# Score products two in a row, then both halves of one maximum product, in the order of TensorE's work

## The reference

```python
q, k, v = x @ Wq + bq, x @ Wk + bk, x @ Wv + bv      # 16 heads of 16 channels
q, k = rope(q), rope(k)
probs = softmax(q @ k.T / 4, axis=-1)                # per head, 2048 x 2048
x = layernorm(x + probs @ v)
r = sigmoid((mu_r * x + (1 - mu_r) * x_prev) @ W_r.T)
k = (mu_k * x + (1 - mu_k) * x_prev) @ W_k.T
out = layernorm(x + r * (square(relu(k)) @ W_v.T))   # x_prev: x one token earlier
```

## Time and profile before

| What | Before |
|---|---|
| Median of three runs | 1656.05 us |
| Profiled execution | 1656.13 us |
| Its span | 1654.3 us |
| TensorE (PE) busy | 1595.5 us, 96% |
| VectorE (DVE) busy | 1443.4 us, 87% |
| ScalarE (ACT) busy | 1168.3 us, 71% |
| Mean granted TensorE clock | 0.975 |

### The profile page before, as it was taken

The page is one execution under the profiler, slowest core; times in us unless marked ns, Lnnn a source line. Parts: engine busy times, 40 slices in busy tenths (PEclk is TensorE's granted clock), DMA queues, the critical chain, the costliest instruction groups (busy, mean ns, idle before and its releaser), DMA issues.

```text
span 1654.3 us, 47865 instructions
## 1 busy us (share of the span) xinstructions
PE 1595.5 (96%) x21312; PEld 683.9 (41%) x21312; DVE 1443.4 (87%) x1491; ACT 1168.3 (71%) x2184; POOL 217.0 (13%) x270
## 2 busy tenths in 40 slices
PE   8858999999999999999999999999999999999997
PEld 4421444444444444444444444444444444443475
DVE  5999888898898898898898998898889989986687
ACT  2441677777777777777777777777777777778542
POOL 4547000000000000000000000000000000001155
PEclk9885899999999999999999999999999999999999
DMA  3344400000000000000000000000000000000011
GB/s 126 114 137 175 129 22 21 22 21 21 21 21 22 21 21 22 21 20 20 18 19 19 17 19 21 21 22 21 21 21 21 21 21 22 2 2 2 1 39 64
DMA packets 36334, 57.70 MB, mean 35 GB/s; under 512 B 5408, under 2 KB 27168, under 8 KB 36128
## 3 DMA queue, kind: packets, MB, share of 16 engines
q1 hardware_dynamic: 34432, 51.53, 9.5%
q10 hardware_dynamic: 1696, 3.12, 0.5%
HBM read 37.46 MB, written 16.78 MB: 33 GB/s over the span
## 4 chain that ended last, share of the span: by engine, by line
PE 85%; DVE 9%; ACT 2%; issue 2%; DMA 1%; SPq 0%; ACTq 0%; POOLq 0%; DVEq 0%; POOL 0%
PE score_ps L547 27%; PE pv_ps L462 27%; PE ring_ps L437 26%; DVE tile_max L938 2%; ACT region L685 2%; DVE ctx_all L879 1%; PE ring_ps L445 1%; DVE region L880 1%; PE score_ps L600 1%; PE ring_ps L511 1%; DMA k_stack<-qk_parts 1%; PE ring_ps L410 1%; DVE ctx_all L878 1%; DVE ctx_all L1013 1%; DVE region L900 1%
## 5 line engine op out<-in xcount | busy, mean ns | idle before, releaser
L938 DVE TENSOR_REDUCE tile_max<-ring_ps 128x1 f32<-128x1024 f32 x1024 | 1207.5, 1220 | 130.6 <-PE ring_ps L437 127.5
L685 ACT ACTIVATE region<-score_ps 128x512 f32<-128x512 f32 x2048 | 1066.9, 602 | 308.1 <-PE score_ps L547 307.5
L437 PE MATMUL ring_ps<-k_stack,q_stack 96*32 96x512 bf16 x8192 | 804.8, 390 | 17.6 <-DMA k_stack<-qk_parts 11.4
L547 PE MATMUL score_ps<-q_stack,k_stack 99*32 99x512 bf16 x8192 | 797.9, 381 | 7.5 <-ACT region L685 3.3
L462 PE MATMUL pv_ps<-region,v_aug 128*32 128x512 f32 x4096 | 529.9, 592 | 0.0
L547 PEld LDWEIGHTS score_ps<-q_stack,k_stack 99*32 99x32 bf16 x8192 | 222.5, 95 | 368.3 <-ACT region L685 183.5
L437 PEld LDWEIGHTS ring_ps<-k_stack,q_stack 96*32 96x32 bf16 x8192 | 219.8, 97 | 356.1 <-DVE tile_max L938 184.7
L462 PEld LDWEIGHTS pv_ps<-region,v_aug 128*32 128x32 f32 x4096 | 125.1, 110 | 103.9 <-ACT region L685 1.6
L813 POOL TENSOR_TENSOR neg_cuts<-neg_max,zeros 128x16 bf16<-128x16 f32 x32 | 7.1, 220 | 888.1 <-DVE neg_max L929 888.1
L410 PE MATMUL ring_ps<-region 128*128 128x512 f32 x128 | 66.5, 674 | 20.0 <-ACT region L651 11.5
L657 ACT ACTIVATE region<-ctx_all 128x2048 bf16<-128x2048 f32 x8 | 15.3, 1910 | 72.4 <-DVE ctx_all L884 52.9
(11 more groups left out here) (70 smaller groups left out, 572.7 us busy)
## 6 DMA issues: line engine op xcount, KB each, us to landing
qk_parts<-region SPq DMA_DIRECT2D x8, 1536.0 KB, 7.5
q_stack<-qk_parts SPq DMA_DIRECT2D x32, 192.0 KB
k_stack<-qk_parts SPq DMA_DIRECT2D x32, 192.0 KB
region<-x_ch SPq DMA_DIRECT2D x8, 512.0 KB, 5.7
q_stack<-qk_parts SPq DMA_DIRECT2D x32, 128.0 KB
k_stack<-qk_parts SPq DMA_DIRECT2D x32, 128.0 KB
region<-x_tok SPq DMA_DIRECT2D x2, 2048.0 KB, 12.6
out<-region SPq DMA_DIRECT2D x8, 512.0 KB, 2.9
```

The costliest lines, as they stand in the source:

```text
L437: mm = pe.matmul(slot[g:g + VCOLS, c * TOK:(c + 1) * TOK], q_stack[0:ROWS, buf, qt * P + g:qt * P + g + VCOLS], k_stack[0:ROWS, buf, lo:lo ...
L547: mm = pe.matmul(score_ps[bank][g:g + VCOLS, :], k_stack[0:ROWS_M, buf, kt * P + g:kt * P + g + VCOLS], q_stack[0:ROWS_M, buf, j * TOK:(j ...
L685: act.activation(probs[:, kt % 2, j, :], score_ps[score_bank(n)[0]][:, :], ACT.Exp, scale=SCALE).then_inc(exps_done, 1)
L938: dve.reduce_max(tile_max[:, parity, unit // 2, unit % 2:unit % 2 + 1], slot[:, :], AX.X)\
```

## The change

The call that issues ring work behind every score product is now made twice behind every second one:

```diff
                         mm.then_inc(scores_ready, 1)
-                        next(work, None)
+                        if j % 2:
+                            next(work, None)
+                            next(work, None)
                         if heads_after == 0:
```

## The result

The changed kernel takes 1687.71 us, the median of four runs (1687.04 to 1687.86), against 1655.98 us for the kernel before. The ratio is 1.0191, with a 95% interval of 1.0173 to 1.0209: slower by 31.7 us. The forecast was 1688.8 us, or 32.8 us slower.

What follows compares the result with a forecast made beforehand. The prediction took TensorE's stream, busy 96% of the span, as the bound. Its terms, 21.8 + 6.6 + 2.3 + 2.1 = 32.8 us, on the profiled 1656.13 us gave 1688.9, or 1688.8 us as a median; range 1682 to 1696.

Steps and rivals of the forecast that it cites:

- The ordinary cycle: 311 cycles without special work: fourth score product waits for the first exponential until 1.15 us; +0.070 us each, 21.8 us.
- Cycle 1: Heads 1 to 30: fourth score product already late, two halves behind it instead of one; +0.219 us each, 6.6 us.
- Cycles 3 and 15: 60 cycles: small wait for VectorE's buffer goes, wait for the exponential comes; +0.038 us each, 2.3 us.
- Cycle 14: 30 heads: first half behind "neg" still waits for VectorE, then the fourth score product is late; +0.070 us, 2.1 us.
- Cycle 13: Third score product has four groups before it in either order and the rest behind it; no change.
- Cycle 2: Transposes delay the score products; the half needing their buffer is due at 611.35, buffer free at 611.33; no cost.
- The maxima's DMAs: Three DMAs issued one group later, landing at most 3.0 us after issue: hidden; if not, 6.6 us in all.
- the score product was not on time: Rival: fourth score product on time, only cycle 1 pays, cycles 3 and 15 gain; 1660.9 us, chance 0.03.
- the ring's waits: Rival, faster: halves' 1.8 us of waits for VectorE go; with 7.7 us from like products, 1646.5 us, chance 0.03.
- exponentials 0.03 us late across the board: Rival: exponential starts at 0.53 us in all 401 gated cycles; 12 us more, 1700.8 us, chance 0.05.
- Like products in a row: Part of the faster rival: score products in a row start 0.004 us closer; 7.7 us gained, chance 0.03.
- The clock stayed at 1.00: Rival: short gaps make TensorE's clock fall to half; 21 us per affected head, 1710 us and up, chance 0.02.

Runs made afterwards that it cites:

- (0, 2, 2, 0): Against the kernel before, 0, 2, 2 and 0 halves issued behind the four score products, the fourth behind all halves: 1655.45 us, ratio 0.9994.
- (0, 1, 0, 3): Against the kernel before, 0, 1, 0 and 3 halves issued behind the four score products: 1791.49 us, ratio 1.0823.

## Why the prediction was right, step by step

- **The ordinary cycle.** Forecast 2.678 us, measured 2.673; the fourth score product at 1.15 us was exact. The 0.005 too much comes from what stands behind it. I had added two halves at 0.219 us, 0.438 together, to the last head's 2.24. In the nanoseconds of the trace they take 0.220 and 0.215, together 0.435, and the rest of the cycle 0.860 instead of 0.862. (The working's 8 x 0.219 + 0.86 is 2.612 and not 2.608, a rounding on which nothing rests.) Over head 20 that is 0.065 us a cycle above, by the medians of all heads 0.066: 311 x 0.066 = 20.5 us, not 21.8. This is the term that was mis-sized.
- **Cycle 1.** One group more behind the gated product: 2.91 us, 0.217 more than before, 6.5 us for 6.6.
- **Cycles 3 and 15.** The small wait for VectorE went and the gate came, 2.672 us or a little more. In nanoseconds of the timeline that is 0.027 above the old 2.646, 1.6 us for the 2.3 forecast from rounded rows.
- **Cycle 14.** 2.89 for 2.82 us: 2.1 us, as forecast. **Cycle 13:** unchanged, as forecast.
- **Cycle 2.** "Nothing, but by a hair": it took 3.306 us, 0.005 more. The half comes when VectorE has just freed its buffer, and the two experiments that moved a half forward there paid 0.22 us (0, 2, 2, 0) and 0.16 us (0, 1, 0, 3).
- **The maxima's DMAs.** They did not stay hidden in every head. Over the whole run the first weight load of a head waited for them eight times, up to 1.04 us, and three times the head's first score product came late, by 0.05, 0.1 and 0.3 us; in the kernel before none did. The costliest, where the value product starts at 1406.33 and the next head 1.17 us later instead of 0.86:

```profile
1407.50 0.12 PEld L547 LDWEIGHTS score_ps<-q_stack,k_stack 99*32 99x32 bf16 x8 [1.04 <-DMA q_stack<-neg_rows]
```

The step "they land at most 3.0 us after issue" was read from one head; over all heads the longest took 4.2 us, in both kernels. It cost 0.5 us of the 6.6 that the prediction named as the price. That the later "neg" product is what made them late was not tested by itself.

The terms above the DMAs sum to 30.7 us, against 30.9 in the span. What the forecast didn't have nearly cancels, in the two recorded executions. On the one side, five times in the run the first exponential starts 0.28 us late. The cause was not looked for. The kernel before has them in the same cycles. There the fourth score product has 0.16 us in hand, and such a cycle takes 0.13 us more; here the whole 0.28 comes through. That holds for four of them, 4 x 0.15 = 0.6 us; the fifth falls in a cycle 13, where a score product waits in both kernels. Added to it are the 0.5 us of the DMAs and 0.2 us in one cycle of the last head. On the other side, cycle 1 of head 0 was 0.55 us shorter, since the clock rose to 1.00 at 175.1 us of the span and not at 176.9; the attention began 0.4 us sooner; and the cycles 13 were 0.3 us shorter together.

The rivals: the score product was not on time (it starts 1.15 us behind the first in the median of every ordinary cycle, released by the exponential); the ring's waits did shrink, but off the path, so that nothing was gained; exponentials 0.03 us late across the board didn't come: of the 300 ordinary cycles of heads 1 to 30, 296 have it within 0.51 us of their start. Like products in a row do save a little, 0.007 us a cycle for two pairs, about the rate that the prediction gave them; it decides nothing here. The clock stayed at 1.00 through the attention once it had risen in head 0, with a gap in nearly every cycle. The Trainium skill, "TensorE: Matmul & The Clock Gate", section "A second HAM failure mode: psum-queue depth-cycling", reports of another kernel that frequent small idle spells between groups of matmuls made the clock swing. That didn't happen here: with gaps of 0.07 us a cycle the granted clock is 1.00, and so it is in the (0, 1, 0, 3) run, where TensorE stood 0.28 us in each cycle (1.00 from 180 to 1500 us).

## What to carry to other kernels

In an order written out by hand, each product that reuses a buffer has a due time and a release time; work out both from the cycle's start, and count the groups ahead of it (they set its due time) and behind it (they pay if it is late). A loop without stalls may still have a margin of 0.16 us somewhere, and moving one group of 0.22 us uses it up in every pass. Put the gated products late in their cycle, and work out the same for every buffer that the moved work needs, in the odd cycles too.

## What the runs showed of the hardware that I had not expected

- Which of two waits an instruction carries itself, and which stands ahead of it alone, followed the order in which they were asked for (the exponential carries the one asked for first), and it was worth 0.06 us: the exponential started 0.50 us behind its score product with the scores' wait standing alone, and 0.44 with the value product's wait standing alone. On a loop without slack this was 25 us.
- The group behind two groups of the same kind, be it of that kind or of the other, starts 0.215 us behind the second of them; otherwise groups that don't wait lie 0.218 to 0.220 apart (medians of the traces), the two of a pair too. With three pairs in a cycle it gave up to 0.01 us in a cycle of 2.6 (2.597 against 2.607). Why was not looked for.
